# A fused transformer kernel: the last sequence's first scores ahead of the last down product, and its tap copies, tanh, table load, combined tiles and scaled tiles in another order

## The reference

```python
xn = layernorm(x)
s  = attention(xn)           # rope, 2 query heads, 1 key head, causal softmax
g  = silu(moe(xn))           # 8 experts, top 2: gate * (gelu(xn@wg.T+bg) * (xn@w1.T+b1)) @ w2.T + b2
x  = x + s * g
xn = layernorm(x)
h  = rmsnorm(xn) * norm1_w
local = causal_depthwise_conv(h, conv_w)      # 7 taps
decay = clip(sigmoid(h @ Wdecay + bdecay), .05, .95);  gate = sigmoid(h @ Wgate + bgate)
state = cumsum(gate * h / max(shifted_cumprod(decay), 1e-7)) * cumprod(decay) * state_scale
mem   = ((h @ Wk) @ M.T) @ Wmem * mem_scale
mixed = xn + concat(local, state, mem) @ Wc + bc
s  = mixed + (silu(h2 @ Wg) * (h2 @ Wup)) @ Wdown      # h2 = rmsnorm(mixed) * norm2_w
g  = silu(tanh(xn @ W1 @ W2 @ W3 + bias))
x  = x + s * g
```

## Time and profile before

| what | value |
|---|---|
| median of 3 runs | 528.92 us |
| the profiled execution | 530.34 us |
| its span | 528.5 us |
| PE busy | 515.4 us (98%) |
| DVE busy | 389.8 us (74%) |
| ACT busy | 314.4 us (59%) |
| POOL busy | 235.1 us (44%) |

### The profile page before, as it was taken

One profiled execution on the slowest core, in us unless ns is written; L12 is line 12 of the kernel. 1 busy time (PEld: TensorE's weight loads), 2 busy tenths in 40 slices (PEclk: granted clock), 3 DMA queues, 4 the chain that ended last, 5 costly groups with the idle time before them and its releaser, 6 DMA issues. The chain is left out here.

```text
span 528.5 us, 12881 instructions
## 1 busy us (share of the span) xinstructions
PE 515.4 (98%) x3193; PEld 387.5 (73%) x3194; DVE 389.8 (74%) x1106; ACT 314.4 (59%) x830; POOL 235.1 (44%) x245
## 2 busy tenths in 40 slices
PE   9999999999999999999999999998999999999997
PEld 5756667677779999999999999976445545554544
DVE  6659778977886777767776777757788888788654
ACT  5635555555657666666666666657776657656511
POOL 4434766666631333333333333344476647523310
PEclk9999999999999999999999999999999999999999
DMA  7930133335528656556565655519100000000001
...
DMA packets 85268, 54.01 MB, mean 102 GB/s; under 512 B 53088, under 2 KB 70016, under 8 KB 85104
## 3 DMA queue, kind: packets, MB, share of 16 engines
...
...
## 5 line engine op out<-in xcount | busy, mean ns | idle before, releaser
L1894 ACT ACTIVATE AR<-bank,BGT 128x128 f32<-128x128 f32 x284 | 81.3, 369 | 69.4 <-PE bank L928 69.4
L637 POOL DMA_INDIRECT rows_y<-YO,W1E x71 | 69.0, 972 | 118.0 <-DVE YO L1408 115.0
L1425 DVE SCALAR_TENSOR_TENSOR AR<-bank,B1T,AR 128x128 f32<-128x128 f32 x284 | 80.1, 344 | 3.4 <-ACT AR L1894 2.1
L601 POOL DMA_INDIRECT slots_x<-XR,SLOT x64 | 64.0, 1000 | 35.9 <-DMA slots_x<-XR,SLOT 19.5
L946 PE MATMUL bank<-W2E,AR 128*128 x568 | 75.1, 275 | 0.5 <-DVE AR L1425 0.5
L928 PE MATMUL bank<-AR,WGE 128*128 128x128 f32 x568 | 75.1, 275 | 0.0
L937 PE MATMUL bank<-AR,WGE 128*128 128x128 f32 x568 | 75.0, 275 | 0.0
L946 PEld LDWEIGHTS bank<-W2E,AR 128*128 128x128 f32 x568 | 69.1, 192 | 0.7 <-issue 0.7
L937 PEld LDWEIGHTS bank<-AR,WGE 128*128 128x128 f32 x568 | 69.1, 192 | 0.0
L928 PEld LDWEIGHTS bank<-AR,WGE 128*128 128x128 f32 x568 | 69.1, 192 | 0.0
L1799 ACT ACTIVATE AR<-bank,AR 128x512 f32<-128x512 f32 (+1 forms) x64 | 33.8, 528 | 53.2 <-DVE AR L1330 53.1
...
## 6 DMA issues: line engine op xcount, KB each, us to landing
...
```

The costliest lines, as they stand in the source:

```text
L601: pool.indirect_dma_start(out=slots_x, out_offset=bass.IndirectOffsetOnAxis(ap=SLOT[:, k, n:n + 1], axis=0), in_=XR[:, n, :], in_offset=No ...
L637: pool.indirect_dma_start(out=rows_y, out_offset=bass.IndirectOffsetOnAxis(ap=DST[:, j:j + 1], axis=0), in_=YO[q % 2][:], in_offset=None). ...
L1425: s = dve.scalar_tensor_tensor(out=HT[u][:, c, :], in0=B[3 + u][:, c * P:(c + 1) * P], scalar=B1T[:, bass.ds(e, 1), c], in1=ZB[u][:, c, :] ...
L1894: act.activation(ZB[u][:, c, :], B[1 + u][:, c * P:(c + 1) * P], ACT.Gelu, bias=BGT[:, bass.ds(e, 1), c]).then_inc(c_gelu, 1)
```

## The change

On TensorE the scores of step 0 of the last sequence are issued ahead of the last down product. The wait for the last output (`c_yo`) with five constant matmuls behind it goes; a wait for the last sum (`c_sum`) stands two steps in. Behind the last step eight constant matmuls become three, and the waits for `pt_done` and `o_done` go (the second is now ahead of `d_step(0)`). The four transposes of the scaled tiles wait for one tile each; `d_hs` counts four for sequence 0, so the helper `scaled_tiles` gives the later counts.

On VectorE the maximum of step 0 stands ahead of the last output. The sum of the expert rows and its product (`d_first_both`, `d_first_product`) move to behind the first `combine`, in step 5. The gate of sequence 1 (`d_early_gate(1)`) and the mean (`d_first_mean_scaled`) change places with their neighbours. On ScalarE the four tap copies, which stood ahead of the attention, are done one in each of its first four steps; the two tanh move from steps 4 and 6 to 5 and 7; the table load and `d_front2(2)` move to behind `d_turned(0)`. On GpSimd `scales(1)` goes ahead of `front(2)`.

```diff
--- before
+++ after
@@ -374,6 +374,10 @@
+def scaled_tiles(b):
+
+    return TPS + b
+
 def half_tiles(half):
@@ -659,7 +663,7 @@
             pool.wait_ge(d_xn, b)
-            pool.wait_ge(d_hs, b)
+            pool.wait_ge(d_hs, scaled_tiles(b - 1))
         if b == 0:
@@ -701,8 +705,8 @@
     pool.wait_ge(d_nmr, 1)
+    scales(1)
     front(2)
-    scales(1)
     for b in range(NSEQ):
@@ -855,14 +859,14 @@
         for k in range(NS):
-            scores(b, u, k)
+            if not (last and k == 0):
+                scores(b, u, k)
             if b == 0 and k == 2:
...
                 project(b + 1, 1 - u, PROJECT_AT[b == 0].index(k))
-            if last and k == 1:
-                pe.wait_ge(c_yo, SLOT_TILES)
-                keep_warm(0, 5)
+            if last and k == 2:
+                pe.wait_ge(c_sum, SLOT_TILES)
             if not (first and k < 1):
@@ -969,17 +973,20 @@
         c_step(j, j % 2, j % WBUFS)
+    scores(NB, NB % 2, 0)
     pe.reg_load(e_down, TEXP[0:1, SLOT_TILES - 1:SLOT_TILES])
...
     def d_turn_scaled(b):
-        pe.wait_ge(d_hs, b + 1)
         if not (isinstance(b, int) and b == 0):
+            pe.wait_ge(d_hs, scaled_tiles(b))
             pe.wait_ge(d_ht, b)
...
         for i in range(TPS):
+            if isinstance(b, int) and b == 0:
+                pe.wait_ge(d_hs, i + 1)
             mm = pe.transpose(B[1][:, i * P:(i + 1) * P], HS1[:, i, :], ident)
@@ -1147,7 +1154,6 @@
-    pe.wait_ge(c_ht, SLOT_TILES)
     attend(NB, NB % 2, first=True, last=True)
@@ -1155,13 +1161,12 @@
     pe.wait_ge(exp_done, NS * NSEQ)
-    keep_warm(3, 8)
-    pe.wait_ge(pt_done, NS * NSEQ)
-    pe.wait_ge(o_done, TPS * NSEQ)
+    keep_warm(3, 3)
     d_turn_scaled(0)
...
     d_first_conv()
+    pe.wait_ge(o_done, TPS * NSEQ)
     d_step(0, first=True)
@@ -1336,7 +1341,8 @@
         for k in range(NS):
-            row_max(b, k)
+            if not (last and k == 0):
+                row_max(b, k)
             if b == 0 and k == 0:
@@ -1347,12 +1353,13 @@
                 gates()
-            if last and k == 4:
-                d_first_both()
-            if last and k == 5:
-                d_first_product()
             if k in (5, 6):
                 combine(b, k - 5)
+            if last and k == 5:
+                d_first_both()
+                d_first_product()
+            if last and k == 6:
+                d_first_gate()
             if k in (1, 2) and not first:
@@ -1361,11 +1368,8 @@
                 experts((k - 1) // 2)
-            if last:
-                if k == 6:
-                    d_first_gate()
-                if k == 7:
-                    d_stats(0)
+            if last and k == 7:
+                d_stats(0)
@@ -1443,6 +1447,7 @@
         c_step(j, j % WBUFS, last=j == SLOT_TILES - 1)
+    row_max(NB, 0)
     c_out(SLOT_TILES - 1, (SLOT_TILES - 1) % WBUFS, dve.snap(e_last, min_val=0, max_val=E - 1))
@@ -1477,9 +1482,8 @@
         for i in range(TPS):
-            s = dve.tensor_scalar(HS1[:, i, :], X[:, i, :], MV0[:, i, 0:1], RV0[:, TPS + i:TPS + i + 1],
-                                  ALU.subtract, ALU.mult)
-        s.then_inc(d_hs, 1)
+            dve.tensor_scalar(HS1[:, i, :], X[:, i, :], MV0[:, i, 0:1], RV0[:, TPS + i:TPS + i + 1],
+                              ALU.subtract, ALU.mult).then_inc(d_hs, 1)
@@ -1693,11 +1697,11 @@
     d_radicands(0, MV0, VV0)
-    d_early_gate(1)
     finish(NB)
     d_first_scaled()
+    d_early_gate(1)
+    d_first_mean_scaled()
     d_add_x(1)
-    d_first_mean_scaled()
     d_stats(1)
@@ -1854,9 +1858,11 @@
             if last:
-                if k == 4:
+                if k < KEPT:
+                    first_tap(k)
+                if k == 5:
                     d_tanh(0)
-                if k == 6:
+                if k == 7:
                     d_tanh(1)
@@ -1866,7 +1872,8 @@
         head0(b, 3)
-        bring_table(ACT.Gelu if b < NSEQ - 1 else ACT.Silu)
+        if b < NSEQ - 1:
+            bring_table(ACT.Gelu)
@@ -1911,8 +1918,10 @@
     bring_table(ACT.Exp)
-    act.wait_ge(c_wu, SLOT_TILES)
-    for j in range(KEPT):
+
+    def first_tap(j):
+        if j == 0:
+            act.wait_ge(c_wu, SLOT_TILES)
         act.activation(TAPX[:, j, :], W3[:, 2, :], ACT.Copy, scale=VEC[:, V_CONV + j:V_CONV + j + 1]
@@ -2048,18 +2057,17 @@
-    act.wait_ge(c_ht, SLOT_TILES)
-    act.wait_ge(c_y, SLOT_TILES)
     attend(NB, NB % 2, first=True, last=True)
     finish(NB)
-    d_front2(2)
     act.wait_ge(d_zero, 4)
     d_turned(0)
+    bring_table(ACT.Silu)
     d_first_normal(0, 2)
...
     d_gate_affine(0)
+    d_front2(2)
     d_first_normal(2, TPS)
```

## The result

The changed kernel takes 530.33 us (median of 12 runs, 529.71 to 538.21), the kernel before beside it 529.11 (12 runs). The ratio is 1.0028, 95% interval [1.0015, 1.0041]: slower by 0.28%, 1.2 us by the medians and 1.5 by the ratio, outside the forecast's range. (Ratios leave out disturbed runs, medians don't.)

What follows compares the result with a forecast made beforehand. It took a chain of hand-overs between engines at 349 to 380 us as the bound: 1.66 + 0.35 won, 0.87 and 0.88 lost, so -0.26 us, 528.65 from 528.92; own range 528.0 to 529.2, 8 in 10 527.4 to 529.9.

Steps and rivals of the forecast that it cites:

- Step 1: Experts to attention: scores ahead of the last down product start row maximum 0 1.66 us earlier; taps hidden, rows 0.34 later.
- Step 2: Attention steps: late row transfers and VectorE's block of combined tiles leave only 0.79 of the 1.66 us.
- That is hidden: Last weighing, delayed 0.4 us by the second tanh: no cost, as output tiles are needed only when L664 ends.
- The clock rival: Fewer idle matmuls halve TensorE's clock between 368 and 376 us: 1.4 slower, 530.4; chance 0.12.
- the rows as the next limit: At L1463: the second row transfer, taking 4.1 us, lands at 359.95, so the sum waits and starts about 360.0.
- The late-rows rival: First row transfers take 0.5 to 1 us longer, blocking row maximum 6: 529.2 to 529.6; chance 0.12 shared with two others.
- Step 3: Scaled tiles waited for one by one: one transpose left behind the last tile, copy L1938 0.35 us earlier.
- Step 4: ScalarE: table load behind the copy puts L1982 1.40 us behind it; the branch gains only 0.21 us.
- the page's case: Table load plus a drain, 2.66 us per switch: L1982 at 372.29, kernel about 0.9 slower, 529.8; in a shared 0.12.
- Step 5: Silu of rows 2 (0.61 us) ahead of the second L1982 pair: TensorE waits 0.9, L991 starts 0.26 earlier.
- The sum: State product L1037 0.26 us earlier: 1.66 + 0.35 won, 0.87 lost at rows and VectorE, 0.88 at load and silu.
- signs of being wrong: Clock under 1 at 350 to 380; no wait before L991; L1982 over 1.5 us behind L1938; L1037 outside 378.3 to 379.3.

Runs made afterwards that it cites:

- b_best: Kernel before plus early scores, taps, combined tiles, tanh, single scaled tiles, idle matmuls in both gaps, GpSimd's row additions behind first sum and `front(1)`; state +30.97 (before +30.10).
- a_pool2: Changed kernel with GpSimd's `front(2)` product moved behind VectorE's first scan: 530.28 us, ratio 1.0025 to the kernel before.
- a_warm: Changed kernel with all removed idle matmuls put back (five at the scores, eight behind the last step): state at +32.34; its total settles nothing.
- a_again: Changed kernel unedited, profiled a second time: state at +31.96 us (first trace +31.52); its total settles nothing.
- b_scores: Kernel before with only early scores, spread taps, moved combined tiles and tanh, five idle matmuls gone: 530.62 us, ratio 1.0026.
- b_table: Kernel before with only the later table load and silu and the new VectorE and GpSimd orders: state +31.18 us (before +30.10); total settles nothing.

## Why the prediction was wrong

**Step 1 was right.** Row maximum 0 gained 1.77 (1.66 forecast), the last down product and the store came 0.24 and 0.19 later, and the taps cost nothing: row maxima 2 to 4 are 1.9 earlier than before.

**Step 2 failed**, in the sentence that from row maximum 6 on "VectorE has the same work, so L664 on GpSimd starts at 365.73 instead of 366.52". The same work took longer. Row maximum 6 came at +11.96, even before the +12.30 forecast; the power came at +17.34 instead of +16.74, since the sum was held 0.95. Before, GpSimd's addition of sequence 1 ran from +12.50 to +13.98, mostly beside VectorE's row maximum and combining, which read PSUM, and ended 0.09 behind the start of the gate product. After, it started at +13.10, right behind the landing of its rows, and VectorE's sum at +13.46 instead of +14.60. They met. The Trainium skill, "SBUF — State Buffer", section "SBUF: two separate sides", says that a VectorE operation with two inputs in SBUF and a GpSimd one that reads SBUF take one port pair under an exclusive lock for the whole instruction. The traces agree: 1.64 for 0.69, 1.50 for 0.68, 1.22 for 0.14, 1.19 for 0.16, each ending 0.02 to 0.55 behind GpSimd's; and with GpSimd's operation moved away the sum took 0.69 (`b_best`) and L1544 0.14 (`a_pool2`).

The failure doesn't hang on the one trace: with the scores ahead, eleven of twelve traces have an operation of VectorE held ahead of the power, the sum with X or a 128x4 one of the statistics; with the old order two of six, the gate product. And it could have been read before the run. The trace of the kernel before has such holds of its own in the last stage: at 437.38 the statistics operation L1523, else 0.16, takes 1.20 beside GpSimd's L656, which started at 437.29 and takes 1.27.

"That is hidden", said of the last weighing, failed next. With the clock halved it ended at 366.99, and the scaled tiles began at +19.46 instead of +18.21. The power had ended at +18.38, and at its usual 1.56 the weighing would have ended 0.94 earlier; so the fall cost about 0.9, an estimate from these rows that no run isolates. The clock rival had named the mechanism, but at another place, another price and from another cause: 1.7 us between 368 and 376 by the idle matmuls taken out. The fall came between 364 and 368, and in `a_warm`, which put those matmuls back, the clock fell too. What was new was a standstill behind a late VectorE. I read the earlier trace rows for what was taken from TensorE and not for what an order on another engine would take from it. Of eight traces with standstills of 1.85 or more in sum, seven fell; none of the ten others did, among them all five with idle matmuls ahead of the last turn. The length alone doesn't decide: 1.81 and 1.06 were kept in `a_again` and fallen in `b_scores`.

The same step had the rows as the next limit, by the 4.1 us of the second transfer. In the first trace it took 3.12, and L1468 started at +10.64 without a wait, where +11.0 with one was forecast. The late-rows rival was right in kind (L1468 to +12.02) and had its reason wrong: the second transfer took 3.39 in `a_again`, less than before, and the issue was late.

**Step 3 was right and too small:** from the first scaled tile to the copy 1.59 instead of 2.09, 0.50 won where 0.35 was forecast. But that the branch through L651 "keeps its old times" was wrong: the second sum came at +22.54 instead of +21.28, and 0.52 later even in `b_table`.

**Step 4 was right:** 1.42 from the copy's end to the first normals. The Trainium skill, "ScalarE: Activation LUTs", section "What ACT_TABLE_LOAD costs", has a drain of 1.38 beside the load; the trace of after shows none at this switch either. For the page's case the prediction's own numbers give 0.98 (1.24 less 0.26) and not the 0.9 that it says.

**Step 5 was right on ScalarE and wrong on VectorE.** Copy to transposes was 6.78 (6.88 forecast). But the silu releases GpSimd's `front(2)`, which the step gave no price, and it fell exactly beside L1544: 1.08 on the scan, of which the state product saw 0.58.

**The sum:** state forecast at +29.84, measured +31.52. 1.10 of the 1.68 is the copy (held sum and clock, less 0.15 won by the tiles), 0.58 the held mean. The end followed the state, 149.0 to 149.7 later in all traces, as said. Two of the signs of being wrong that the prediction had named are in the trace: a granted clock under 1 between 350 and 380, and the state product too late.
